# Dividing by the softmax sums after the product with V, with the sums made on TensorE, in a two-layer attention and experts kernel

## The reference, cut to what matters

```
xw = windows of 64 tokens of the normalized x
q, k, v = split(xw @ qkv_w.T + qkv_b);  q, k rotated, q scaled
attn = softmax(einsum('bhnd,bhmd->bhnm', q, k), axis=-1)
out  = einsum('bhnm,bhmd->bhnd', attn, v)
x = x + out @ proj_w.T + proj_b
```

## Time and profile before

| | |
|---|---|
| median of 3 executions | 967.04 us (962.99, 967.04, 967.79) |
| profiled execution | 976.7 us, of which the span is 974.9 us |
| PE busy | 661.1 us, 68% of the span |
| DVE, POOL, ACT busy | 450.5, 422.3, 351.3 us |
| mean granted clock of TensorE | 0.844 of full speed |
| attention, from the first `S` to the last of its work | about 33 to 350 us |
| first experts layer, whitening, second experts layer | to about 574, 640 and 975 us |

### The profile page before, as it was taken

One profiled execution on the slowest core, in us unless ns is written; L12 is line 12 of the kernel. 1 busy time (PEld: TensorE's weight loads), 2 busy tenths in 40 slices (PEclk: granted clock), 3 DMA queues, 4 the chain that ended last, 5 costly groups with the idle time before them and its releaser, 6 DMA issues.

```text
span 974.9 us, 17268 instructions
## 1 busy us (share of the span) xinstructions
PE 661.1 (68%) x5696; PEld 465.0 (48%) x5696; DVE 450.5 (46%) x1258; ACT 351.3 (36%) x861; POOL 422.3 (43%) x417
## 2 busy tenths in 40 slices
PE   2777887878878675666888848882363565678770
PEld 0345555545445454554555536661253354556550
DVE  1676668665753435222343338465221634334444
ACT  1556554543432333332454424241131232234440
POOL 3454444473461345554333332035362274554440
PEclk9899989897976776886999979995585787779995
DMA  6000699992000211222333132001203311525407
GB/s 259 22 13 13 103 160 160 158 158 47 18 21 10 54 36 52 58 54 80 103 105 103 49 124 63 1 1 33 65 32 62 55 44 45 105 60 118 93 29 260
DMA packets 81207, 73.76 MB, mean 76 GB/s; under 512 B 9264, under 2 KB 70841, under 8 KB 80737
## 3 DMA queue, kind: packets, MB, share of 16 engines
q1 hardware_dynamic: 71792, 54.51, 27.4%
q0 software_dynamic: 8896, 17.47, 5.6%
q10 hardware_dynamic: 432, 0.68, 0.2%
HBM read 35.37 MB, written 38.16 MB: 75 GB/s over the span
## 4 chain that ended last, share of the span: by engine, by line
PE 24%; issue 19%; DVE 5%; DMA 4%; ACT 3%; another core or an unknown queue 3%; POOL 3%; SPq 1%; POOLq 0%; ACTq 0%; DVEq 0%
PE bank L1292 6%; PE bank L1277 4%; PE bank L1279 3%; PE bank L1278 3%; PE bank L1284 2%; PE bank L1325 1%; DMA fetched<-results 1%; PE bank L1259 1%; DVE xl L909 1%; DVE X L956 1%; DMA results<-work,rowbuf 1%; PE bank L1327 1%; DMA spare<-b_dram 1%; PE bank L1145 1%
## 5 line engine op out<-in xcount | busy, mean ns | idle before, releaser
L608 POOL DMA_INDIRECT results<-work,rowbuf x142 | 138.4, 975 | 215.9 <-ACT work L750 87.2
L915 DVE SCALAR_TENSOR_TENSOR work<-work,rowbuf,bank 128x256 f32<-128x256 f32 x142 | 68.1, 480 | 203.0 <-ACT work L740 145.8
L1277 PE MATMUL bank<-Wh,xl 128*128 x142 | 78.1, 550 | 100.0 <-DVE xl L909 37.1
L1292 PEld LDWEIGHTS bank<-W,work 128*128 128x128 f32 x568 | 94.3, 218 | 55.0 <-issue 45.1
L1292 PE MATMUL bank<-W,work 128*128 x568 | 104.8, 314 | 21.8 <-ACT work L745 13.6
L1145 PE MATMUL bank<-half 128*128 128x384 bf16 x484 | 109.9, 376 | 9.2 <-DVE work L922 6.3
L740 ACT ACTIVATE work<-bank 128x256 f32<-128x256 f32 x142 | 54.5, 384 | 155.5 <-PE bank L1279 92.3
L1277 PEld LDWEIGHTS bank<-Wh,xl 128*128 128x128 f32 x142 | 30.4, 214 | 121.9 <-issue 121.9
L1145 PEld LDWEIGHTS bank<-half 128*128 128x128 bf16 x484 | 52.1, 112 | 44.7 <-issue 16.6
L622 POOL DMA_INDIRECT region<-rows_a,where x64 | 63.3, 989 | 22.9 <-issue 20.4
L553 POOL TENSOR_TENSOR rstd_m<-var_m,C 128x4 f32<-128x4 f32 x16 | 16.5, 1034 | 112.5 <-DVE var_m L812 112.5
(11 more groups left out here) (230 smaller groups left out, 1262.9 us busy)
## 6 DMA issues: line engine op xcount, KB each, us to landing
region<-pad SPq DMA_DIRECT2D x16, 1040.0 KB
rowbuf<-region SPq DMA_DIRECT2D x142, 65.0 KB
fetched<-results SPq DMA_DIRECT2D x16, 512.0 KB, 4.5
spare<-w1gv_dram SPq DMA_DIRECT2D x8, 640.0 KB
spare<-b_dram SPq DMA_DIRECT2D x71, 64.0 KB
results<-work,rowbuf POOLq DMA_INDIRECT x142
work<-w_dram SPq DMA_DIRECT2D x8, 256.0 KB, 2.7
W<-w_dram SPq DMA_DIRECT2D x2, 1024.0 KB, 12.0
```

Source lines behind the costliest of these rows:

```text
L608: pool.indirect_dma_start(results[layer], bass.IndirectOffsetOnAxis(ap=at, axis=0), ysb[:, T % YRING, :], None, bounds_check=PAIRS - 1, oo ...
L915: v.scalar_tensor_tensor(out=hh[:, i % 2, :], in0=sg[:, i % 2, :], scalar=rowbuf[:, i % RING, GATE_AT:GATE_AT + 1], in1=bank[:, b, FF:2 * FF],
L1277: mm(bank[:, b, :], low, wh, start=True, stop=False)
L1292: last = mm(bank[:, b, 0:P], hT[:, i % 2, ft * P:(ft + 1) * P], W2[layer][:, bass.ds(experts[i] * FT + ft, 1), :].rearrange("p a n -> p (a ...
```

## The change

`norm` and `sum` go. `PT` waits for `exp` itself, and `warm` in front of it goes. Behind the 32 matmuls of `O`, 16 matmuls with a new constant `head_ones` (64x32 of ones and zeros, 128 columns streamed) put the sums of each head into the other columns of bank 2, each repeated over the 8 channels of its head. DVE takes the reciprocal of these 128x128 sums and multiplies the product by it (`divide`), where ACT had copied it. `PT` and `O` stand a step earlier, `J` too; `route` and `gates` move by half a step, so do `place` and its DVE part, and `put` moves by one.

```diff
-              "Q1": -1, "Kb1": -1, "V0": 0, "Vm0": 1, "V1": 2, "Vm1": 3, "J": 7, "J_add": 7, "stats1": 7, "rows": 8, "turn": 9}
-UNIT_STEP = {"logits": 10, "route": 11, "gates": 11, "place": 12, "list": 13}
-PIECE_STEP = {"S": -1, "max": 0, "sub": 0, "exp": 0, "sum": 1, "norm": 1, "PT": 2, "O": 3}
-PUT_STEP = 12
+              "Q1": -1, "Kb1": -1, "V0": 0, "Vm0": 1, "V1": 2, "Vm1": 3, "J": 6, "J_add": 7, "stats1": 7, "rows": 8, "turn": 9}
+UNIT_STEP = {"logits": 10, "route": 11.5, "gates": 11.5, "place": 12.5, "list": 13}
+PIECE_STEP = {"S": -1, "max": 0, "sub": 0, "exp": 0, "PT": 1, "O": 2, "divide": 2.5}
+PUT_STEP = 13
...
-            if name == "norm":
-                pool.wait_ge(p_rec, i + 1)
-                pool.tensor_tensor(p, p, srec[:, i % BT, :].unsqueeze(2).to_broadcast([P, HEADS, WIN]), ALU.mult)\
-                    .then_inc(p_nrm, 1)
...
-            if name == "O":
-                k, b = i % BT, wait_full(act, "O", i)
-                act.activation(on(i // BT)[:, k * P:(k + 1) * P], bank[:, b, 0:P], ACT.Copy).then_inc(free("O", i), 1)
...
-            if name == "sum":
-                v.tensor_reduce(ssum[:, i % BT, :], sx(i).rearrange("p (h m) -> p h m", h=HEADS), AXIS_X, ALU.add)\
-                    .then_inc(p_sum, 1)
-                v.reciprocal(srec[:, i % BT, :], ssum[:, i % BT, :]).then_inc(p_rec, 1)
+            if name == "divide":
+                k, b = i % BT, wait_full(dve, "O", i)
+                v.reciprocal(sums[:, i % 2, :], bank[:, b, P:2 * P]).then_inc(o_rec, 1)
+                dve.wait_ge(o_rec, i + 1)
+                v.tensor_tensor(on(i // BT)[:, k * P:(k + 1) * P], bank[:, b, 0:P], sums[:, i % 2, :], ALU.mult)\
+                    .then_inc(free("O", i), 1)
...
-                warm(b, WARM_PIECE)
-                pe.wait_ge(p_nrm, i + 1)
+                pe.wait_ge(p_exp, i + 1)
...
+                for j in range(4):
+                    for q in range(2):
+                        for hh_ in range(2):
+                            r, o = slice(64 * hh_, 64 * hh_ + 64), 32 * (2 * hh_ + q)
+                            last = mm(bank[o:o + 32, b, P:2 * P], con("head_ones")[r, j * 32:(j + 1) * 32],
+                                      PT[r, 4 * q + j, :], start=(j == 0), stop=(j == 3))
```

More of the change, by code:

```diff
@@ L52, in constants @@
         "minus_half": np.full((P, BT), -0.5),
+        "head_ones": np.broadcast_to((ch[None, :] // 32 == ch[None, :] % 32 // HD), (P, P)),
         "first_wins": np.broadcast_to(E - e[None, :], (P, E)),
@@ L114 @@
 RAW_AT = 35
-WARM_PIECE, WARM_BLOCK, WARM_CHAIN = 8, 6, 3
+WARM_BLOCK, WARM_CHAIN = 6, 3
 COV_STEP = {"sum0": 0, "c_stats": 0, "yc": 1, "yturn": 2, "mean": 2, "cov": 3}
@@ L127 @@
 ORDER = ("up", "Vm0", "Vm1", "O", "S", "J", "V0", "V1", "dn", "out", "xt", "ht",
-         "a_y", "Kb0", "Kb1", "rows", "route", "white", "max", "sub", "J_add", "stats1", "a_stats", "Q_turn", "K_turn", "sum", "exp",
-         "Q0", "Q1", "norm", "yc", "sum0", "T", "turn", "logits", "gates", "place", "list", "put",
+         "a_y", "Kb0", "Kb1", "rows", "route", "white", "max", "sub", "divide", "J_add", "stats1", "a_stats", "Q_turn", "K_turn", "exp",
+         "Q0", "Q1", "yc", "sum0", "T", "turn", "logits", "gates", "place", "list", "put",
          "PT", "Q", "K", "split", "fold_w", "fold", "c_stats", "yturn", "mean", "cov")
@@ L287, in build @@
         cov_acc = sb("cov_acc", [P, P])
-        smax, ssum, srec = (sb(n, [P, BT, HEADS]) for n in ("smax", "ssum", "srec"))
+        smax = sb("smax", [P, BT, HEADS])
         stats = {n: sb(f"stats_{n}", [P, BT, 6]) for n in "amc"}
@@ L329, in build @@
             PT = asb("PT", [P, HP, P])
+            sums = asb("sums", [P, 2, P])
             Vm = asb("Vm", [P, BW, 4, HP * HD])
@@ L382, in build @@
         q_t, q_m, k_t, k_r, k_bd, v_sb = (sem(n) for n in ("q_t", "q_m", "k_t", "k_r", "k_bd", "v_sb"))
-        s_half, s_max, p_exp, p_sum, p_rec, p_nrm, x_bias = (sem(n) for n in (
-            "s_half", "s_max", "p_exp", "p_sum", "p_rec", "p_nrm", "x_bias"))
+        s_half, s_max, p_exp, o_rec, x_bias = (sem(n) for n in ("s_half", "s_max", "p_exp", "o_rec", "x_bias"))
         mean_row, means_set = sem("mean_row"), sem("means_set")
@@ L578, in pool_step @@
                 pool.tensor_tensor(kr, tk[:, 0, :], tk[:, 1, :], ALU.add).then_inc(k_r, 1)
-            if name == "norm":
-                pool.wait_ge(p_rec, i + 1)
-                p = sx(i).rearrange("p (h m) -> p h m", h=HEADS)
-                pool.tensor_tensor(p, p, srec[:, i % BT, :].unsqueeze(2).to_broadcast([P, HEADS, WIN]), ALU.mult)\
-                    .then_inc(p_nrm, 1)
             if name == "stats1":
@@ L870, in dve_step @@
                     .then_inc(free("S", i), 1)
-            if name == "sum":
-                dve.wait_ge(p_exp, i + 1)
-                v.tensor_reduce(ssum[:, i % BT, :], sx(i).rearrange("p (h m) -> p h m", h=HEADS), AXIS_X, ALU.add)\
-                    .then_inc(p_sum, 1)
-                dve.wait_ge(p_sum, i + 1)
-                after(dve, p_nrm, i - BT + 1)
-                v.reciprocal(srec[:, i % BT, :], ssum[:, i % BT, :]).then_inc(p_rec, 1)
+            if name == "divide":
[4 more added lines that the diff above has]
+                    .then_inc(free("O", i), 1)
             if name == "J_add":
```

## The result

The changed kernel takes 997.69 us (median of 4 runs, 990.47 to 1004.38) against 967.14 of the kernel before beside it: ratio 1.032, interval 1.024 to 1.041. It is slower, where 961 us was forecast. The execution profiled of it took 1000.23 us.

What follows compares the result with a forecast made beforehand. PE was taken to bound a plain block, at 31.3 us. The terms -14 - 2 + 16 - 9 + 1 + 5 - 3 gave -6 us, a median of 961 us from 967.04, with an 8 in 10 range of 942 to 982.

Steps and rivals of the forecast that it cites:

- PE, forecast -14 us: PE's work per piece in the attention: unread matmuls out, ones matmuls in; -14 us, ends -6 and -24.
- The clock, forecast +5: Attention: the new wait before `V1` brings some 7 us of low clock in each of two blocks; +5 us.
- the bound named: Attention clock: the forecast is wrong if it leaves 0.80 to 0.90.
- the second rival: Attention: without unread matmuls the clock falls, the low quarter becomes a half; +30 us, 991 us; chance 0.23.
- The sign named for the plain block: Profile after: plain block near 31 us if the clock holds, near 34 if it falls once.
- `V1` behind `J_add`, forecast +16: Both use bank 3, so PE stands 2.3 us before `V1` until `J_add` empties it, seven times; +16 us.
- The first rival: The wait at `V1` doesn't show, taking time PE would have stood anyhow; 945 us, or 935; chance 0.22.
- `O` behind `divide`, forecast as hidden: The next `O` waits for `divide` to free bank 2; PE's 3.5 us of other work covers its 1.24 us.
- `route`, forecast -9: `route` behind `max` and `sub`: 3 us of 6.3 given back, three times; -9 us.
- `place`, `list` and the port, +1: Three DVE waits for POOL's `norm` go, -5 us; `place` and `list` delay a `divide`, +6; together +1 us.
- Where the experts begin, forecast -3: Start of the experts: 6 us gained between first `xt` and first `dn`, less two `put`s behind `out`; -3 us.

Runs made afterwards that it cites:

- `b_nwones`: Kernel before without the 8 unread matmuls ahead of each `PT`, with the ones matmuls behind each `O`, their sums unread: 984.31 us, ratio 1.010.
- `b_nowarm`: Kernel before without the 8 unread matmuls ahead of each `PT`, nothing else changed: 966.25 us, ratio 0.997.
- `a_pt2pnd`: Changed kernel with the piece steps of before, `place` earlier, and no divide (ACT copies the product, sums unread): 997.8 us, ratio 1.031 to the kernel before.
- `a_warm`: Changed kernel with the 8 unread matmuls put back ahead of each `PT`: 1023.39 us, ratio 1.055 to the kernel before.
- `a_fill`: Changed kernel with 8 unread matmuls issued just before each of the 7 later `V1`: 998.81 us, ratio 1.027 to the kernel before.
- `a_pt2r`: Changed kernel with `PT`, `O`, divide and `J` at the steps of before, `route` and `gates` at 11: 1012.7 us, ratio 1.043 to the kernel before.
- `a_noones`: Changed kernel without the ones matmuls, the reciprocal reading the product itself (division by the sums left out): 969.96 us, ratio 1.003 to the kernel before.

## Why the prediction was wrong

**PE, forecast -14 us.** This term failed, with the largest part of the miss that a run shows. Each instruction took what was forecast: the ones add 0.9 to 1.0 us to an `O` at full clock, the unread group had its 1.30. Even the difference was: in `b_nwones` PE is busy for 12.0 us less. What failed is the step from there to the time of the kernel, that PE bounds the blocks, so that what leaves its list leaves the kernel. PE idles for 24 us more in `b_nwones`, waiting longer for ACT and standing inside its own groups of matmuls, and the kernel is slower by 10 to 15 us. The sum also left the clock where it was, a quarter of the stretch low. The unread matmuls had held it: without them and without the ones the clock of the stretch is 0.75, and the 42 us that leave PE's list shorten the kernel by 3. The ones bring it back to 0.85 and cost 13 to 20 us. So -14 became +10 to +15.

**The clock, forecast +5.** The changed kernel's stretch is at 0.79, 0.01 under the bound named, so the second rival was the nearer one: 991 us with half of the attention low, and it is 42% low (twice the 0.21 that 0.79 lacks). Its mechanism was right and is not the whole, as the 1023 us at a clock of 0.88 show. The rule of the Trainium skill named there (TensorE: Matmul & The Clock Gate, "What's actually happening"), that activity releases the fast clock, agrees with the four clocks by the number of unread matmuls, 0.88 down to 0.75; it does not give the time, which hardly followed them. How much is the clock? The runs of one kernel differ in time with it. The four spans of the changed kernel are 988.6 us at 0.832, 993.3 at 0.821, 998.4 at 0.818 and 1002.5 at 0.812, about 0.7 us for each thousandth. A straight line through all executions gives 1.0 for the ten of `b_nwones`, 0.8 for the 25 of the kernel before beside it, 0.6 for the 13 of the kernel before in the first experiments and for the ten of `b_nowarm`, and 0.1 for the four of `a_pt2pnd`. Between the profiled executions of before and after lie 26 thousandths: by 0.6 to 1.0 us each, 16 to 26 us, against the 23.5 measured. That is an estimate by correlation; a wait can lower the clock as well, and with the stretch at the same clock `a_warm` is slower than the kernel before by 5.5%. The sign named for the plain block, about 31 us if the clock holds and about 34 if it falls once, came out: 31.12 us at 1.00 in `a_fill`, 34.00 and 34.37 at 0.90 in the changed kernel.

**`V1` behind `J_add`, forecast +16.** The wait is there (14.2 us with the seventh instance, 2.1 each, forecast 2.3), and no run found it worth its length: with `J` behind it, and with unread matmuls in it, the time is the same within the intervals. In the first of these the waits of `O` grew by 4 us, and in the second PE is kept busy by other means, so its price alone is not shown. The first rival, that it stands in time that PE loses anyhow, is not refuted by this; the gain it forecast did not come.

**`O` behind `divide`, forecast as hidden.** It is, in a plain block (no wait in the timeline there). Behind `place` and `list` it is not. Moving `list`, which took that wait away, or taking out the divide altogether gave nothing that can be told from zero. The divide cost 0.96 and 0.29 us, as forecast.

**`route`, forecast -9, and `place`, `list` and the port, +1.** The idle time moved from `route` to `place`, and the blocks there are 7.2, 11.6 and 14.0 us longer than before. Putting `place` earlier, and `list` behind a divide with it, gave 1.9% in one pair of kernels, 1.3% in another and at the median 0.8% in a third, relative to the runs beside each; in the last two `J_add` moved too. So a better order was worth 8 to 19 us, where this one was to gain 8 in all. The long operations of DVE also stayed in part: the one of `place` is gone (0.29 us at worst, 1.96 before), but beside the three long ones of `list` above POOL ran these.

```profile
194.68 1.27 POOL L579 TENSOR_TENSOR tk<-tk 128x512 f32<-128x512 f32 x1 [17.80 <-DVE tk L819]
195.91 0.72 POOL L576 TENSOR_TENSOR Q<-tq 128x256 f32<-128x256 f32 x1
...
199.29 1.27 POOL L569 TENSOR_TENSOR X<-X,att_bias 128x512 f32<-128x512 f32 x1
```

Each ends within 0.1 us of the operation of DVE beside it (195.97, 196.65, 200.66). Without `norm` others stand in its place.

**Where the experts begin, forecast -3.** From the last `max` to the end the span is 3.6 us shorter, and the first `dn` comes 17.5 us behind the first `xt` (358.86, 376.31; forecast 16). The size agrees; the cause isn't shown, since the rest of the span is 5.6 us longer than before in `a_pt2r`, which has the steps of before (666.8 us from the last `max`, against 661.2 before and 657.6 in the changed kernel).

**The sum.** In ratios: unread matmuls out, -0.3%; ones in, +1.3% or more; together 1.010 to 1.016. Taken from the other side, out of the changed kernel, the ones are worth 2.9%. From the 1.010 to the 1.032 of the changed kernel, the order around `place` is 0.8 to 1.9%. The divide is worth from nothing to 0.7%, and the steps of the pieces nothing that is good. What is left shows in part as a lower clock under the same work, and in part at an equal mean clock. Why stays open; no run here set it apart from the order of the items.

## What to carry to other kernels

An unread matmul is not free time that waits to be taken: before counting its length as a gain, run the kernel with none and with half of them. Here none gave 0.3% (perhaps nothing), half gave 1.0%, and the work that replaced them cost more than either. A shorter list of PE's is not a shorter kernel: PE's busy time fell by 12 us in `b_nwones` and its idle time rose by 24. Where PE bounds a stretch at 80% busy, count its work at the clock that will be there and not at that of the trace, and count a wait removed at zero until another wait behind it is ruled out. An item that waits for PE (`place`) should not stand ahead, on its engine, of one for which PE waits (`divide`).

## What the runs showed of the hardware that was not expected

One kernel's time varied by 1.4% (the changed kernel) to 2.8% (`b_nwones`) with the granted clock of the same execution, 0.7 and 1.0 us for each thousandth of it; in `a_pt2pnd` it hardly did (0.1). Four unread matmuls of 384 columns for each piece held the attention at 0.85, eight at 0.88, two at 0.80, none at 0.75. The ones matmuls, which use 64x32 places of the array, held it too, but not alike in both kernels: in the order of before they raised it from 0.75 to 0.85 (`b_nowarm`, `b_nwones`), as four unread ones did, and in the changed kernel from 0.75 to 0.79 (`a_noones`), where four unread ones beside them raised it to 0.82. So the same matmuls went with different clocks in two orders; why is not shown. PE stood for up to 4.78 us inside one group of matmuls (`b_nwones`, 170.20 us) with nothing in the profile that it waited for.
